# Last feed-forward chunk in halves, its rounding on VectorE and GpSimd, root's table earlier, two fold copies behind the first roots

## What is computed

```
x = x + relu(batch_norm(local_attention_7x7(group_norm(x))))
t = tokens(x)
t = t + attn(ln(t))     # 8 heads; only the diagonal of the softmax weights is used:
                        # av = attn[b,n,n,h] * v[b,n,:,h];  out = av.reshape(b,n,1024) @ W0 + b0
t = t + ffn(ln(t))      # router per image picks 2 of 8 experts (softmax, capacity, softmax, top 2)
# ffn: h = gelu(x @ W1[e] + b1[e]);  y = h @ W2[e] + b2[e];  out = sum of w_e * y_e
#      return layer_norm(out + x) * gamma + beta
```

## Time and profile before

| | us |
|---|---|
| median of 3 runs | 399.25 |
| the profiled execution | 399.49 |
| its span, first to last instruction | 397.8 |
| PE busy | 382.7 (96%) |
| DVE busy | 314.1 (79%) |
| ACT busy | 275.4 (69%) |
| POOL busy | 152.9 (38%) |

### The profile page before, as it was taken

One profiled execution on the slowest core, in us unless ns is written; L12 is line 12 of the kernel. 1 busy time (PEld: TensorE's weight loads), 2 busy tenths in 40 slices (PEclk: granted clock), 3 DMA queues, 4 the chain that ended last, 5 costly groups with the idle time before them and its releaser, 6 DMA issues.

```text
span 397.8 us, 5816 instructions
## 1 busy us (share of the span) xinstructions
PE 382.7 (96%) x1902; PEld 301.0 (76%) x1902; DVE 314.1 (79%) x710; ACT 275.4 (69%) x528; POOL 152.9 (38%) x206
## 2 busy tenths in 40 slices
PE   8899999999999999999998999999999999998994
PEld 3678895777888888888886888888877767645772
DVE  2798947688998998898998898899898165657745
ACT  1567666687698888888878888888886201557880
POOL 7400005297355645325514469667400000225015
PEclk9999999999999999999999999999999999999999
DMA  7990000000000000000001900000000000000002
GB/s 270 368 351 10 0 2 0 3 0 0 2 1 0 2 1 2 1 0 2 0 2 38 386 4 1 0 2 2 2 0 0 2 0 2 0 0 1 2 0 105
DMA packets 5263, 15.52 MB, mean 39 GB/s; under 512 B 690, under 2 KB 1906, under 8 KB 4978
## 3 DMA queue, kind: packets, MB, share of 16 engines
q1 hardware_dynamic: 4802, 14.19, 9.8%
q10 hardware_dynamic: 432, 0.97, 0.7%
HBM read 14.08 MB, written 1.08 MB: 38 GB/s over the span
## 4 chain that ended last, share of the span: by engine, by line
PE 81%; DVE 9%; ACT 6%; issue 2%; POOLq 0%; POOL 0%; DVEq 0%; ACTq 0%
PE ps L1186 13%; PE ps L1188 13%; PE ps L1187 13%; PE ps L1280 7%; DVE nmax_all L1668 3%; PE ps L1168 3%; PE ps L919 3%; PE ps L1170 3%; PE ps L1169 3%; PE ps L1062 3%; PE ps L1099 2%; PE ps L1106 2%; PE ps L1028 2%; PE ps L1051 1%; ACT conv_e L892 1%
## 5 line engine op out<-in xcount | busy, mean ns | idle before, releaser
L1668 DVE TENSOR_REDUCE nmax_all<-ps 128x1 f32<-128x1024 f32 x128 | 156.2, 1220 | 18.1 <-PE ps L1188 17.2
L790 ACT ACTIVATE exps<-ps,nmax_all 128x1024 bf16<-128x1024 f32 x128 | 142.6, 1114 | 35.8 <-DVE diag_all L1673 34.7
L1186 PE MATMUL ps<-qT_hi,kT_hi 128*128 128x512 f32 x256 | 103.3, 403 | 0.3 <-ACT exps L790 0.3
L1188 PE MATMUL ps<-qT_hi,kT_lo 128*128 128x512 f32 x256 | 100.8, 394 | 0.0
L1187 PE MATMUL ps<-qT_lo,kT_hi 128*128 128x512 f32 x256 | 100.4, 392 | 0.0
L1188 PEld LDWEIGHTS ps<-qT_hi,kT_lo 128*128 128x128 f32 x256 | 48.1, 188 | 10.8
L1186 PEld LDWEIGHTS ps<-qT_hi,kT_hi 128*128 128x128 f32 x256 | 48.1, 188 | 10.7 <-ACT exps L790 3.1
L1187 PEld LDWEIGHTS ps<-qT_lo,kT_hi 128*128 128x128 f32 x256 | 48.2, 188 | 7.5 <-issue 0.2
L530 POOL CAST qT_hi<-xq 128x341 fp32r<-128x341 f32 (+1 forms) x45 | 21.1, 469 | 83.1 <-ACT xq L772 82.0
L532 POOL TENSOR_TENSOR qT_lo<-xq,qT_hi 128x341 fp32r<-128x341 f32 (+1 forms) x45 | 41.6, 925 | 3.6
L1673 DVE CUSTOM_DVE_ANT_0 diag_junk<-ps,ident 128x128 f32<-128x128 f32 x128 | 35.8, 280 | 0.0
(11 more groups left out here) (234 smaller groups left out, 650.3 us busy)
## 6 DMA issues: line engine op xcount, KB each, us to landing
xs_first<-a_store SPq DMA_DIRECT2D x4, 512.0 KB, 5.5
xs_second<-a_store SPq DMA_DIRECT2D x4, 512.0 KB, 8.4
wqkv<-laid_qkv_weights SPq DMA_DIRECT2D x1, 1536.0 KB, 6.7
wvT<-laid_qkv_weights_T SPq DMA_DIRECT2D x1, 1536.0 KB, 10.1
xq<-laid_x_queries SPq DMA_DIRECT2D x2, 512.0 KB, 6.3
xk<-laid_x_keys SPq DMA_DIRECT2D x2, 512.0 KB, 7.7
x<-in_x SPq DMA_DIRECT2D x1, 1024.0 KB, 13.0
w<-in_L_ffn_W SPq DMA_DIRECT2D x1, 1024.0 KB
```

The costliest lines, as they stand in the source:

```text
L790: a.activation(exps[:, n % 2, :], slot(score_slot(col)), ACT.Exp, bias=nmax_all[:, col:col + 1], accum_out=sum_all[:, col:col + 1]).then_i ...
L1186: mm(tgt, keys_hi, qT_hi[:, u % 2, at], start=True, stop=False)
L1188: last = mm(tgt, keys_lo, qT_hi[:, u % 2, at], start=False, stop=True)
L1668: v.tensor_reduce(nmax_all[:, col:col + 1], slot(place), AX_X, ALU.max, negate=True)\
```

## The change

Its parts, in the order of the program:

1. `take_folded(4)` and `take_folded(5)` move on ScalarE from ahead of the first squares to behind the first two roots. The second spread of norm 0 goes into bank 3, and TensorE's wait for all six folds moves behind that spread.
2. In the loop, ScalarE squares chunks 0 and 1 behind gelu 3 and 5 (before: 4 and 6, and chunk 2 behind gelu 7); TensorE makes variances 0 and 1 behind `hidden(6)` and `hidden(7)`.
3. For the last pair, n = 7, ScalarE no longer rounds: VectorE rounds half 0, GpSimd half 1 (semaphores `h_last`).
4. Root's table is loaded right behind the last gelu, and the square of chunk 2 comes behind root 0.
5. Chunk 3 goes in halves of 256 tokens: residual, square, diagonal, spread, normalisation, add and DMA.
6. On TensorE the first spread comes ahead of the last variance, and the seven fillers go.
7. VectorE normalises chunk 0 ahead of the last reciprocal, and adds chunk 2, too; GpSimd adds chunks 0 and 1, once both halves of the last diagonal are laid.

The diff:

```diff
--- before.py
+++ after.py
@@ -297,2 +297,3 @@
         h_ps, h_full, h_sb, h_lo, y_ps = (sem(n) for n in ("h_ps", "h_full", "h_sb", "h_lo", "y_ps"))
+        h_last = [sem(f"h_last{f}") for f in range(2)]
         b2_centred, w2_mean_ready, w2_centred = (sem(n) for n in (
@@ -303,3 +304,5 @@
         last_diagonal = sem("last_diagonal")
-        out_ready = [sem(f"out_ready{c}") for c in range(4)]
+        out_ready = [sem(f"out_ready{c}") for c in range(5)]
+        HALVES = (1536, 1792, 2048)
+        LAST_HIDDEN = 7
 
@@ -435,8 +438,6 @@
             of = out.rearrange("b c h w -> c b (h w)")
-            for n in range(4):
+            for n, (lo, hi) in enumerate(zip((0, 512, 1024) + HALVES[:2], (512, 1024, 1536) + HALVES[1:])):
                 sp.wait_ge(out_ready[n], 1)
-                b, half = n // 2, n % 2
-                sp.dma_start(of[:, b, half * 512:(half + 1) * 512],
-                             conv_o[:, n * 512:(n + 1) * 512]).then_inc(out_sem, 16)
-            sp.wait_ge(out_sem, 64)
+                sp.dma_start(of[:, lo // HW, lo % HW:lo % HW + hi - lo], conv_o[:, lo:hi]).then_inc(out_sem, 16)
+            sp.wait_ge(out_sem, 80)
 
@@ -607,2 +608,7 @@
 
+            n, f = LAST_HIDDEN, 1
+            pool.wait_ge(h_full, 2 * n + f + 1)
+            pool.wait_ge(y_ps, n - 1)
+            g.tensor_copy(hid_hi[:, n % 2, f, :], hid[:, n % 2, f, :]).then_inc(h_last[f], 1)
+
             for c in range(3):
@@ -611,3 +617,4 @@
 
-            for c in range(3):
+            pool.wait_ge(last_diagonal, 2)
+            for c in range(2):
                 pool.wait_ge(LN[2]["out"], c + 1)
@@ -717,3 +724,3 @@
                 a.activation(third, third, ACT.Relu, scale=st[:, 30:31], bias=st[:, 31:32]).then_inc(bn_relu, 1)
-            for n in range(1, FOLD_BANKS):
+            for n in range(1, 4):
                 take_folded(n)
@@ -743,2 +750,4 @@
             root(0, 1, 0)
+            take_folded(4)
+            take_folded(5)
 
@@ -893,2 +902,4 @@
                                  bias=b1s[:, b, k, f:f + 1]).then_inc(h_full, 1)
+                    if n == LAST_HIDDEN:
+                        continue
                     act.wait_ge(h_full, 2 * n + f + 1)
@@ -901,8 +912,11 @@
                 gelu(n)
-                if n in (4, 6):
-                    square(2, n // 2 - 2)
-            square(2, 2)
+                if n in (3, 5):
+                    square(2, n // 2 - 1)
             load_table(ACT.Sqrt)
             root(2, 0, 6)
-            square(2, 3)
+            square(2, 2)
+            for half in range(2):
+                act.wait_ge(LN[2]["centred"], 4 + half)
+                at = slice(HALVES[half], HALVES[half + 1])
+                a.activation(squares[:, at], centred[:, at], ACT.Square).then_inc(LN[2]["square"], 1)
             root(2, 1, 7)
@@ -1121,5 +1135,5 @@
             spread(0, 0, 7)
-            pe.wait_ge(f_m_sb, 6)
             pe.wait_ge(LN[0]["diagonal"], 2)
-            spread(0, 1, 4)
+            spread(0, 1, 3)
+            pe.wait_ge(f_m_sb, 6)
             centred_product(3, 5)
@@ -1369,3 +1383,6 @@
                 for f in range(FC):
-                    pe.wait_ge(h_sb, 2 * n + f + 1)
+                    if n < LAST_HIDDEN:
+                        pe.wait_ge(h_sb, 2 * n + f + 1)
+                    else:
+                        pe.wait_ge(h_last[f], 1)
                     pe.wait_ge(h_lo, 2 * n + f + 1)
@@ -1386,13 +1403,20 @@
                     hidden(n + 2)
-                if n in (4, 6):
-                    variances(2, 0, 6, n // 2 - 2)
+                if n in (4, 5):
+                    variances(2, 0, 6, n - 4)
             variances(2, 1, 7, 2)
-            keep_warm(3, 4)
-            variances(2, 2, 0, 3)
-            keep_warm(3, 3)
-            for c in range(3):
+            pe.wait_ge(LN[2]["diagonal"], 1)
+            spread(2, 0, 1)
+            for i in range(4):
+                pe.wait_ge(LN[2]["square"], 4 + i // 2)
+                at = HALVES[0] + i * P
+                last = mm(bank(0, i * WIDE, (i + 1) * WIDE), squares[:, at:at + P], mean_w[:, 0:WIDE],
+                          start=True, stop=True)
+            last.then_inc(LN[2]["var"], 1)
+            for c in (1, 2):
                 pe.wait_ge(LN[2]["diagonal"], c + 1)
                 spread(2, c, 1 + c)
-            pe.wait_ge(last_diagonal, 1)
-            spread(2, 3, 4)
+            for half in range(2):
+                pe.wait_ge(last_diagonal, half + 1)
+                mm(bank(4 + half, 0, 256), ones[:, :], diagonal[:, 3, half * 256:(half + 1) * 256],
+                   start=True, stop=True).then_inc(LN[2]["spread"], 1)
 
@@ -1617,3 +1641,3 @@
             take_centred(2, 6)
-            normalise(0, 1, 4, xn)
+            normalise(0, 1, 3, xn)
             take_centred(3, 5)
@@ -1856,3 +1880,10 @@
                 for f in range(FC):
-                    dve.wait_ge(h_sb, 2 * n + f + 1)
+                    if n < LAST_HIDDEN:
+                        dve.wait_ge(h_sb, 2 * n + f + 1)
+                    else:
+                        if f == 0:
+                            dve.wait_ge(h_full, 2 * n + 1)
+                            dve.wait_ge(y_ps, n - 1)
+                            v.tensor_copy(hid_hi[:, n % 2, f, :], hid[:, n % 2, f, :]).then_inc(h_last[f], 1)
+                        dve.wait_ge(h_last[f], 1)
                     if n >= 2:
@@ -1869,2 +1900,9 @@
 
+            def last_residual(half):
+
+                dve.wait_ge(y_ps, 8)
+                lo, hi = HALVES[half:half + 2]
+                v.scalar_tensor_tensor(centred[:, lo:hi], bank(5, lo - HALVES[0], hi - HALVES[0]), b2sum[:, 1:2],
+                                       xn[:, lo:hi], ALU.add, ALU.add).then_inc(LN[2]["centred"], 1)
+
             hidden_remainder(0)
@@ -1875,17 +1913,27 @@
                     hidden_remainder(2 * c + 2)
+                    residual(c)
+                    hidden_remainder(2 * c + 3)
                 else:
                     reciprocals(2, 0)
-                residual(c)
-                if c < 3:
-                    hidden_remainder(2 * c + 3)
+                    for half in range(2):
+                        last_residual(half)
             reciprocals(2, 1)
-            reciprocals(2, 2)
-            lay_diagonal(2, 3, last_diagonal)
             normalise_last(0, 1)
-            normalise_last(1, 2)
-            normalise_last(2, 3)
-            normalise_last(3, 4)
-            dve.wait_ge(LN[2]["out"], 4)
-            at = slice(3 * 512, 4 * 512)
-            v.tensor_tensor(conv_o[:, at], centred[:, at], x1[:, at], ALU.add).then_inc(out_ready[3], 1)
+            reciprocals(2, 2)
+            dve.wait_ge(LN[2]["rstd"], 3)
+            for half in range(2):
+                v.tensor_tensor(diagonal[:, 3, half * 256:(half + 1) * 256].rearrange("p (i n) -> p i n", i=2),
+                                ident[:, :].rearrange("p (i n) -> p i n", i=1).broadcast_to([P, 2, P]),
+                                rstd[:, 12 + 2 * half:14 + 2 * half].rearrange("p (i n) -> p i n", n=1)
+                                .broadcast_to([P, 2, P]), ALU.mult).then_inc(last_diagonal, 1)
+            for c in range(1, 3):
+                normalise_last(c, 1 + c)
+            for half in range(2):
+                dve.wait_ge(LN[2]["spread"], 4 + half)
+                at = slice(HALVES[half], HALVES[half + 1])
+                v.scalar_tensor_tensor(centred[:, at], centred[:, at], VEC["L1_ffn_gamma"], bank(4 + half, 0, 256),
+                                       ALU.mult, ALU.mult).then_inc(LN[2]["out"], 1)
+            for n, (lo, hi) in enumerate(((1024, 1536), HALVES[:2], HALVES[1:])):
+                dve.wait_ge(LN[2]["out"], n + 3)
+                v.tensor_tensor(conv_o[:, lo:hi], centred[:, lo:hi], x1[:, lo:hi], ALU.add).then_inc(out_ready[n + 2], 1)
```

More of the change, by code:

```diff
@@ L1121, in _ @@
             spread(0, 0, 7)
+            pe.wait_ge(LN[0]["diagonal"], 2)
+            spread(0, 1, 3)
             pe.wait_ge(f_m_sb, 6)
-            pe.wait_ge(LN[0]["diagonal"], 2)
-            spread(0, 1, 4)
             centred_product(3, 5)
@@ L1875, in _ @@
                     hidden_remainder(2 * c + 2)
+                    residual(c)
+                    hidden_remainder(2 * c + 3)
                 else:
                     reciprocals(2, 0)
-                residual(c)
-                if c < 3:
-                    hidden_remainder(2 * c + 3)
+                    for half in range(2):
+                        last_residual(half)
             reciprocals(2, 1)
+            normalise_last(0, 1)
             reciprocals(2, 2)
-            lay_diagonal(2, 3, last_diagonal)
-            normalise_last(0, 1)
-            normalise_last(1, 2)
-            normalise_last(2, 3)
-            normalise_last(3, 4)
-            dve.wait_ge(LN[2]["out"], 4)
-            at = slice(3 * 512, 4 * 512)
```

(3 more changed lines are left out.)

## The result

The changed kernel takes 396.83 us, the median of 4 runs (396.73 to 397.15), against 399.23 for the kernel before in 4 runs of the same chip (399.19 to 399.42): 2.40 us less, ratio 0.9941, interval 0.9929 to 0.9953. The forecast was 396.8. The profiled execution took 396.79, with a span of 395.0; that of the kernel before took 399.49.

A forecast was written before the change was run, and what follows sets the result against it. TensorE (81% of the chain) was taken as the bound, with ScalarE's copies at the front and serial steps at the end. Terms 0.37 + 2.08 = 2.45 gave 397.04 profiled from 399.49, median 396.8, range 396.2 to 397.9.

The forecast's parts named there:

- The front: Norm 0: two fold copies moved behind the first roots let the first square and variance start 0.37 us earlier; bounds 0 to 0.39.
- Rival A: Score stage: the front's gain is taken up before the end, price 0.37 us, giving 397.15; chance 0.13.
- The last activations: Last pair: rounding moved from ScalarE to VectorE and GpSimd completes TensorE's last output product only 0.10 us earlier.
- Rival D: Last pair: GpSimd's cast, blocked by 0.5, takes 1.04 and makes the remainder late, 0.45 us more, 397.25; chance 0.05.
- Root's table: Table load at the end runs under TensorE's output products, so the residual starts at 385.40 instead of 386.03.
- The last chunk: Steps from residual to last DMA: spreads overlap root and diagonal, last DMA issued at 393.13 instead of 395.21, 2.08 us won.
- Rival B: Final adds: GpSimd's adds starve VectorE's as before, about 1.1 us more, giving 397.9; chance 0.12.
- The transfers: Output DMAs: five instead of four, the last with half the bytes, landing 2.0 us after issue; change counted as 0.
- Rival C: Output DMAs: the transfers become the bound, 0.7 us more, giving 397.5; chance 0.07.
- rival E: End: without fillers TensorE's granted clock falls to 1.2 GHz before the last variance, about 4.5 us more, 401.3; chance 0.02.

The follow-up runs named there:

- kernel 1: The kernel before with only the fold part: copies 4 and 5 behind the first two roots, second spread in bank 3; 398.88 us, ratio 0.9989.
- kernel 9: The changed kernel with VectorE rounding both last hidden halves and no cast on GpSimd; 396.76 us, ratio 0.9939.
- kernels 4: The changed kernel with ScalarE rounding the last hidden halves again, root's table still ahead of the square of chunk 2; 397.67 us, ratio 0.9957.
- 12: The changed kernel with ScalarE rounding the last hidden halves and squaring chunk 2 ahead of root's table; 398.09 us, ratio 0.9972.
- kernel 10: The kernel before with chunk 0's spread ahead of the last variance, its normalisation ahead of the last reciprocal, three later fillers gone; 398.89 us, ratio 0.9992.
- kernel 11: The kernel before without the three fillers behind the last variance, the four ahead of it kept; 399.24 us, ratio 1.0001.
- kernel 5: The changed kernel with chunk 3 whole, in 512 columns instead of halves; 396.75 us, ratio 0.9937.
- kernel 3: The kernel before without all seven filler matmuls in the last norm; 399.33 us, ratio 1.0001.
- 7: The changed kernel with the first spread behind the last variance and no fillers; 397.50 us, ratio 0.9958.
- kernel 6: The changed kernel without GpSimd's wait for the last diagonal ahead of its two adds; 397.05 us, ratio 0.9946.
- kernel 8: The changed kernel with chunk 3's diagonal laid by ScalarE instead of VectorE and no wait ahead of GpSimd's adds; 396.18 us, ratio 0.9928.

## Why the prediction was right

The mechanism held, and the time was right by more than luck: each term below was found in the trace at about its size. That the last tenth agrees as well is luck: misses of up to 0.2 stand against each other at the end.

**The front** was sized as it came: 0.37 worked out, square and variance of kernel 1 at 64.30 and 64.95, 0.43 by the medians. Rival A, that something takes it up, is refuted by the unchanged wait (0.51 at 89.83).

**The last activations.** The product complete 0.10 earlier: TensorE's variance behind it starts at 384.52 instead of 385.31, 0.79 of which 0.70 are the front and the offset. The casts were off both ways and it did not matter: VectorE's 0.43 (I took 0.49), GpSimd's 0.94 (0.61). GpSimd's came in the middle of VectorE's remainder, which has two operands in SBUF. By the Trainium skill, "SBUF — State Buffer", section "Who interferes with whom", the two exclude each other; the trace agrees, 0.94 against the 0.504 of a cast of 384. As computed, the remainder (over at 383.48) was still in time: TensorE asks for it at 383.83, behind the passes of half 0. Rival D, which had this cast so late that it costs 0.45, is refuted; kernel 9, without the cast, is no faster.

**Root's table.** Hidden, as said; the residual started 0.60 earlier net (0.63 forecast). The account was thin on what each piece is worth: it gave 0.10 to the moved rounding by way of TensorE, and did not say that the rounding is what makes room on ScalarE for table, root and square. The sum is right, since each was worked out with the others in place, but kernels 4 and 12 show that without the moved rounding 0.84 or 1.26 is lost.

**The last chunk.** Diagonal at 387.82; the forecast's 388.47 less 0.70 is 387.77. From there to the end of VectorE's last add it took 4.56 (387.82 to 392.38); worked out were 4.66 (388.47 to 393.13). Its first add was held for 0.42 (1.11 against 0.69), at most 0.45 in the forecast. Rival B (1.1 more) did not happen. In kernels 10 and 11, where GpSimd keeps the third add, the collision is there; no run gives that add back to GpSimd in the changed kernel, so that its move is what spares this one is argued and not shown. Two things that the last-chunk term counts in are worth nothing by themselves: the halves (kernel 5) and taking the fillers out (kernels 3 and 11; they only have to give way to the spread).

What the pieces are worth, each by taking it out of the changed kernel: the spread's place 0.67, the wait ahead of GpSimd's adds 0.22, the rounding 0.84, the halves nothing. They are not a sum, since they lean on each other. Three pieces were never taken out alone: the third add on VectorE, the earlier squares of chunks 0 and 1, and the table's place with the rounding moved.

**The transfers.** They were counted at 0. The last was issued at 392.61, against 393.13 less 0.70, so 0.18 later than worked out, although VectorE was done 0.05 sooner. The wait is for SyncE, still busy with the issue of the first half until 392.56, which the prediction did not count. The last half landed 2.0 after its issue, where the last chunk before took 2.1, which gives some 0.1 back. Rival C (0.7) is refuted.

**The clock** stayed at 1.00; rival E is true of kernel 3 only, and there the median did not move (399.33 against 399.31).

## What to carry to other kernels

At a serial end, list for each engine what stands in its queue between the last product and the last DMA, and move one engine's work into another's wait: a table load under the products, the first chunk's spread ahead of the last statistic, an operand (here the diagonal) on the engine that idles, even if it takes longer there. Count GpSimd's work in SBUF and VectorE's operations with two SBUF operands as one resource, and decide by that which add goes to whom. When an edit removes a block on one side, look for what it gives or takes on the other. Let useful work take the place of fillers where it can; before taking fillers out without a substitute, look at the granted clock behind them.

## What the runs showed of the hardware

- The granted clock after an idle TensorE: in kernel 3, with 1.13 idle, it fell only when TensorE had been at work again for some 1.6, and read 0.50 for three stretches of 1 us; in kernels 11, 7 and 12, with 0.27, 0.19 and 0.97 idle, it stayed at 1.00. What decides this the runs do not tell; kernels 7 and 12 had no fillers ahead of the gap either.
- Whoever starts second is blocked, VectorE (with two SBUF operands) or GpSimd: VectorE's diagonal of 512 took 1.29 instead of 0.69 (kernel 10), GpSimd's three adds 4.16 instead of 3.71 when one of them came second (kernel 11), its cast 0.94 (the changed kernel). The blocked one takes what the other still has to run, plus its own time, less some 0.15: VectorE's add 1.73 = 1.18 + 0.69 - 0.14 before, 1.11 = 0.56 + 0.69 - 0.14 in the changed kernel, the diagonals 1.54 = 0.93 + 0.76 - 0.15 in kernel 6. VectorE's normalisations, which read one operand from PSUM, were not held up: 0.75 for chunk 2 from 389.08 in kernel 8, wholly beside a GpSimd add, which took its usual 1.27.
- Output transfers of half the size landed 2.0 to 2.2 after their issue, as whole ones did. SyncE took 0.45 to issue one instead of 0.33, but the size need not be the reason: both halves' issues stood right behind another (0.04 after its end), and the one whole chunk's issue that did so too (the last of kernel 11) took 0.43.
- Two executions whose instructions are the same up to that point can lie 0.3 us apart at 60 us, an eighth of the effect studied here. Distances between two traces are to be read from a common point.
